# Nine sequences and seven instead of eight and eight: where a Trainium2 kernel splits its expert routing

## The reference, cut to what matters

```python
x = layernorm(x + attention(x))      # 16 heads of 8, alibi bias, causal, output weights
logits = x @ gate_w.T                # 8 experts
probs = softmax(logits); topw, topi = top_k(probs, 2); topw = topw / topw.sum()
routed = sum over the 2 chosen e of topw_e * (silu(x @ gate_e.T) * (x @ up_e.T)) @ down_e.T
shared = (silu(x @ shared_gate.T) * (x @ shared_up.T)) @ shared_down.T
out = layernorm(x + shared + routed)
```

## Time and profile before

| | |
|---|---|
| median of three runs | 1090.53 us (1090.3 to 1091.83) |
| profiled execution, first to last instruction (nothing is shown of what lies around it) | 1172.6 us |
| first unit of sequence 0 | 61.56 us into the span |
| rounds of sequences 1 to 8 | 36.1 to 36.2 us each |
| round of sequence 9, with the routing | 46.91 us |
| first step of the experts | 655.82 us |
| last step of the experts | 1150.71 us |

### The profile page before, as it was taken

The page is one execution under the profiler, slowest core; times in us unless marked ns, Lnnn a source line. Parts: engine busy times, 40 slices in busy tenths (PEclk is TensorE's granted clock), DMA queues, the critical chain, the costliest instruction groups (busy, mean ns, idle before and its releaser), DMA issues. The chain is left out here.

```text
span 1172.6 us, 27905 instructions
## 1 busy us (share of the span) xinstructions
PE 1049.2 (89%) x9236; PEld 724.0 (62%) x9236; DVE 761.8 (65%) x1861; ACT 738.6 (63%) x1630; POOL 634.6 (54%) x1133
## 2 busy tenths in 40 slices
PE   3999999999999989999997898766879999899993
PEld 1445455555455435454543787666769999899882
DVE  3888888888888888888951484221213334566596
ACT  1167887778777667778786344433336777677653
POOL 1045545545455448778877256655654444455542
PEclk9789999999999989999999899878779999999997
DMA  5233233243333314343321511111212223344343
GB/s 139 68 90 100 77 85 90 76 109 86 84 82 78 107 54 112 94 131 89 93 62 49 216 36 47 59 56 57 60 54 61 64 54 87 88 122 120 113 132 94
DMA packets 123243, 101.84 MB, mean 87 GB/s; under 512 B 18736, under 2 KB 113846, under 8 KB 122450
## 3 DMA queue, kind: packets, MB, share of 16 engines
q1 hardware_dynamic: 113362, 78.18, 25.1%
q0 software_dynamic: 8640, 16.87, 4.5%
q10 hardware_dynamic: 1104, 5.01, 1.1%
HBM read 39.31 MB, written 35.66 MB: 64 GB/s over the span
## 5 line engine op out<-in xcount | busy, mean ns | idle before, releaser
L711 ACT ACTIVATE probs<-scores 128x512 f32<-128x512 f32 x640 | 355.4, 603 | 78.3 <-PE scores L620 73.7
L779 POOL TENSOR_SCALAR_AFFINE_SELECT probs<-probs 128x256 f32<-128x256 f32 (+1 forms) x640 | 223.8, 364 | 180.1 <-ACT probs L711 168.2
L1213 DVE TENSOR_TENSOR e_hid<-e_gate,e_up_ps 128x352 f32<-128x352 f32 (+2 forms) x190 | 106.5, 560 | 259.9 <-ACT e_gate L1488 161.1
L916 DVE TENSOR_REDUCE rowmax<-maxed 128x1 f32<-128x512 f32 (+1 forms) x384 | 246.2, 682 | 33.6 <-PE maxed L603 30.2
L597 PE MATMUL maxed<-kstack,qstack 64*128 64x512 bf16 (+3 forms) x1024 | 232.3, 315 | 15.8 <-DMA kstack<-parts 8.5
L620 PE MATMUL scores<-qstack,kstack 64*128 64x512 bf16 (+3 forms) x1024 | 229.2, 303 | 7.2 <-ACT probs L711 6.2
L1571 POOL DMA_INDIRECT y_tokens<-e_raw,e_row_i x142 | 140.2, 987 | 147.7 <-ACT e_raw L1510 116.1
L636 PE MATMUL pv<-probs,vaug 128*32 128x512 f32 (+3 forms) x2048 | 192.7, 449 | 0.4 <-POOL probs L779 0.4
L916 DVE TENSOR_REDUCE maxB<-maxed 128x4 f32<-128x512 f32 x256 | 165.3, 681 | 20.6 <-PE maxed L603 18.6
L620 PEld LDWEIGHTS scores<-qstack,kstack 64*128 64x128 bf16 x1024 | 68.9, 94 | 160.9 <-ACT probs L711 103.9
L603 PE MATMUL maxed<-causal,halves 64*128 64x128 bf16 (+1 forms) x1280 | 162.1, 212 | 0.0
(11 more groups left out here) (185 smaller groups left out, 1568.5 us busy)
## 6 DMA issues: line engine op xcount, KB each, us to landing
qstack<-parts SPq DMA_DIRECT2D x96, 128.0 KB
kstack<-parts SPq DMA_DIRECT2D x96, 128.0 KB
x_sorted<-zeros SPq DMA_DIRECT2D x16, 580.5 KB
e_xs<-x_sorted SPq DMA_DIRECT2D x142, 64.5 KB
e_raw<-y_tokens SPq DMA_DIRECT2D x64, 128.0 KB
xin<-in_x SPq DMA_DIRECT2D x16, 256.0 KB, 3.2
e_group_in<-x1T_all SPq DMA_DIRECT2D x16, 256.0 KB, 3.0
out<-e_raw SPq DMA_DIRECT2D x64, 64.0 KB
```

The lines of the kernel that those rows point to most:

```text
L711: act.activation(probs[g % 2][:, u * T:(u + 1) * T], scores[st.at(0, SEQ_UNITS, UNITS * g + u) % SB][:], ACT.Exp).then_inc(S["exp_done"], 1)
L779: pool.affine_select(out=view, in_=view, compare_op=ALU.is_ge, fill=0.0, base=0, pattern=pattern, channel_multiplier=-1).then_inc(S["maske ...
L916: dve.tensor_reduce(out, keys, AX.X, ALU.max).then_inc(S["max_taken"], 1)
L1213: dve.tensor_tensor(hid[step % len(hid)][rows, 0:cols], gate[step % 2][rows, 0:cols], up_ps[step % 2][rows, 0:cols], ALU.mult).then_inc(S[ ...
```

## The change

The parts become unequal: the first has nine sequences (36 tiles, 79 slots), the second seven (28 tiles, 63 slots). `CTS`, `STARTS`, `CSLOTS` and `ZEROED` hold the numbers of each part, and the sums stay 64 tiles and 142 slots. The rest follows:

- The routing of the first part moves to the round of sequence 10. Its job is split: `rt` (place 25) makes the totals alone and copies them, `rp` (TensorE 29, VectorE 31) makes the other product and `place`. The pieces between go one after each maximum from the 27th on.
- The 72 scatters of the first part: 13 to a round in the rounds 11 to 15 (65), and seven in the experts' steps 8 to 14, one a step, with the semaphore `x_behind`, for which SP waits ahead of the first slot's load.
- 27 steps of the shared expert stand ahead of the slots and 21 behind them. Tokens of the second part are due at 0.74 a step. Mixing starts at step 120 with one tile in 1.25 steps, and for the second part at step 175.
- In both parts the totals' product now comes first, and the experts' routing chain is over 28 tiles.

```diff
-        33: "pv1", 34: "pv2", 35: "x1t", 36: "pv3", 37: "lg"},
+ "PE": ... 25: "pv2 rt", 26: "pv3", 29: "rp", 30: "pv0", ...     "DVE": ... 25: "rt", 31: "rp m", ...
-ROUTE_AT = 9
-SCATTER_AT = (10, 13)
+ROUTE_AT, COUNTED = 10, 12
+SCATTER_FROM, SCATTERS_A_SEQ = 11, 13
-    "rt": ("placed", 0, 1),
+    "rt": ("routed", 0, COUNTED), "rp": ("placed", 0, 1),
-CT = NTILE // CHUNKS
+CTS = (SPLIT_SEQS * QT, NTILE - SPLIT_SEQS * QT)
+STARTS = (0, CTS[0])
+TOKENS_WITHIN = min((B - SCATTER_FROM) * SCATTERS_A_SEQ, 2 * CTS[0])
+TOKENS_BEHIND = 2 * CTS[0] - TOKENS_WITHIN
...
-    dve.wait_ge(S["prefix_ps"], 2)
-    link(dve.tensor_copy(counts[:], prefix[:, CT * NE:2 * CT * NE].rearrange("p (t e) -> p e t", e=NE)))
-    yield
+    dve.wait_ge(S["prefix_ps"], 1)
+    link(dve.tensor_copy(counts, totals.rearrange("p (t e) -> p e t", e=NE)))
+    yield "counted"
...
+    dve.wait_ge(S["prefix_ps"], 2)
+    dve.tensor_tensor(place, prefix.rearrange("p (t e) -> p t e", e=NE),
+                      running.rearrange("p e t -> p t e"), ALU.add).then_inc(S["placed"], 1)
...
-                    if (n + 1) * 11 // SEQ_UNITS > n * 11 // SEQ_UNITS and scattered[choice] < CT:
-                        scatter(pool, keep, dram, 0, scattered[choice], choice, S["x_scattered"])
+                    if n * SCATTERS_A_SEQ // SEQ_UNITS == (n + 1) * SCATTERS_A_SEQ // SEQ_UNITS:
+                        return
+                    scatter(pool, keep, dram, 0, t, choice, S["x_scattered"])
-                pool.wait_ge(S["x_scattered"], 32 * CT)
+                pool.wait_ge(S["x_scattered"], 16 * TOKENS_WITHIN)
...
-                        for _ in range(8):
-                            next(route, None)
+                        next(route)
...
-                        if n < 12 or n >= 30:
+                        if n < 12 or n >= 26:
                             next(route, None)
...
-MIX = ((PARTED + CSLOT + 24, 3, 2), (PARTED + NSLOT + 6, 3, 4))
+MIX = ((PARTED + CSLOTS[0] + 14, 5, 4), (PARTED + NSLOT + 6, 3, 4))
-WRITES_A_STEP, NORM_TAKES, TOKENS_A_STEP = 1.55, 0.7, 0.92
+WRITES_A_STEP, NORM_TAKES, TOKENS_A_STEP = 1.55, 0.7, 0.74
+BEHIND_FROM = 8
...
+                        if n == 0:
+                            sp.wait_ge(S["x_behind"], 16 * TOKENS_BEHIND)
...
+                    if 0 <= step - BEHIND_FROM < TOKENS_BEHIND:
+                        choice, t = divmod(TOKENS_WITHIN + step - BEHIND_FROM, CTS[0])
+                        scatter(pool, keep, dram, 0, t, choice, S["x_behind"])
```

More of the change, by code:

```diff
@@ L224 @@
 NE = 8
+SPLIT_SEQS = 9
 F = 352
@@ L981, in turns_at, with group_bank @@
     return [(chunk, t) for chunk, (first, steps, turns) in enumerate(MIX)
-            for t in range(-2, CT + NORM_LAG) if first + t * steps // turns == step]
+            for t in range(-2, CTS[chunk] + NORM_LAG) if first + t * steps // turns == step]
 def mixed_at(turn, lag):
     chunk, t = turn
-    return chunk * CT + t - lag if 0 <= t - lag < CT else None
+    return STARTS[chunk] + t - lag if 0 <= t - lag < CTS[chunk] else None
+def group_bank(group):
+    return (group + SPLIT_SEQS) % 2
 def quad_at(turn, lag):
@@ L1002, in writes_by_step @@
         room = min(room + WRITES_A_STEP, 2.5) - NORM_TAKES * sum(quad_at(turn, 1) is not None for turn in turns_at(step))
-        due = 2 * CT if step < PARTED else int(tokens_first + TOKENS_A_STEP * (step - PARTED + 1))
+        due = 2 * CTS[1] if step < PARTED else int(tokens_first + TOKENS_A_STEP * (step - PARTED + 1))
         now = [tokens, results]
-        while room >= 1 and tokens < min(due, 2 * CT):
+        while room >= 1 and tokens < min(due, 2 * CTS[1]):
             tokens, room = tokens + 1, room - 1
@@ L1012, in writes_by_step @@
         assert made - results < YTURN
-    assert (tokens, results) == (2 * CT, NSLOT)
+    assert (tokens, results) == (2 * CTS[1], NSLOT)
     return plan
@@ L1095, in experts @@
         picked_in = [sem(f"picked_in{n}") for n in range(TURN)]
-        out_stored = [sem(f"out_stored{n}") for n in range(TURN)]
+        out_stored = keep["out_stored"]
         CONSTS, EXPERTS_IN = 16, 16 * 4
@@ L1155, in _ @@
                             keep_rest(NE, w)
-                route = routing(dve, S, keep, 1, prefix)
+                route = routing(dve, S, keep, 1, prefix[:, 0:CTS[1] * NE], prefix[:, CTS[1] * NE:2 * CTS[1] * NE])
                 by_expert = [P, NTILE, NE]
@@ L1361, in last_chain @@
                         pe.wait_ge(S["chosen"], 1)
-                        tokens = keep["chosen"][:].rearrange("p t e -> p (t e)")
-                        for m, ones in enumerate((keep["before"], keep["onesb"])):
-                            pe.matmul(x_ps[0][:, m * CT * NE:(m + 1) * CT * NE], ones[:], tokens,
+                        tokens, wide = keep["chosen"][:, 0:CTS[1], :].rearrange("p t e -> p (t e)"), CTS[1] * NE
+                        for m, ones in enumerate((keep["onesb"], keep["before"])):
+                            pe.matmul(x_ps[0][:, m * wide:(m + 1) * wide], ones[:], tokens,
                                       start=True, stop=True).then_inc(S["prefix_ps"], 1)
@@ L1659, in build @@
                  "yraw_last": sb("yraw_last", [P, NQUAD, T])}
+        keep |= {"out_stored": [ctx.enter_context(nc.semaphore(f"out_stored{n}")) for n in range(TURN)]}
         attention(nc, io, dram, keep)
```

180 lines of the change are left out of this document (94 added, 86 removed), and 2 rows, old and new, of the table PLACES.

## The result

The changed kernel takes 1094.26 us in the median of 20 runs (1092.44 to 1102.39); the kernel before took 1091.06 us in 20 runs beside it (1088.38 to 1095.71). The ratio is 1.0041, 95% interval 1.0024 to 1.0057; the medians alone are 3.2 us or 0.29% apart, and four runs of over 1100 us pull the ratio up. On another chip it came out at 1.0034 (1.0016 to 1.0051). The forecast was 1094.1 us.

A forecast was written before the change was run, and what follows sets the result against it. The prediction took TensorE to bound plain attention rounds, GpSimd being nearly full in round 15, and the traced slow stretch to be hardly lost untraced. Its terms summed to +3.6 us, 1094.1 us; range 1091 to 1097, over all cases 1085 to 1100.

The forecast's parts named there:

- Rounds 9 and 10: Attention: round 9 loses the routing (-10.7 us), round 10 gets it (+9.7), net -1.0 us (-3.8 to +1.0).
- the rival with round 10 at its floor: Attention: the spread second half costs no clock, so round 10 grows by 6.9 us, not 9.7: 1091.3 us; chance 0.21.
- the rule behind it: The Trainium skill's clock page, read strictly: TensorE that never stands still keeps 2.4 GHz; no size of its own.
- Rounds 11 to 14: Attention: two to three more scatters a round on GpSimd cost +0.6 us in rounds 11 to 13, +0.4 in round 14.
- Round 15: Last attention round: 13 scatters instead of ten on a GpSimd as good as full, +3.1 us (1.5 to 3.7).
- The end of the block: End of the attention: GpSimd waits for a scatter behind the last mask to land, +1.9 us.
- Experts, steps 8 to 14: Seven scatters put GpSimd some 2 us behind, on an input made two steps ahead: +0.4 us (0 to 3).
- First routed step: Experts: its wait for the last weight half goes, with 27 shared steps ahead: -2.3 us (to 0).
- mixing: Experts: 36 tiles bring a ninth group of norms into the routed steps, +0.5 us (0 to 1).
- Dense stretch: Experts' routed steps: the ring and the load hold nobody in untraced runs before either, 0 us.
- The rival on the other side: Experts: the traced loss in the dense stretch is partly real untraced, -4.7 us at the traced price; chance 0.19.
- GpSimd too full: GpSimd's lag in steps 8 to 14 passes its lead and rounds 11 to 14 wait too: 1099 us; chance 0.14.

The follow-up runs named there:

- first trace of before: The kernel before, unedited, in its first traced execution: span 1172.6 us, with a slow stretch in the experts' steps 24 to 70.
- second trace of before: The kernel before, run once more without an edit for another trace: span 1085.3 us, time 1087.03 us.
- first half spread: The changed kernel with the first 12 routing pieces behind every second of the first 24 maxima: 1097.41 us, ratio 1.0048 to the kernel before.
- four together: The changed kernel with experts' scatters in steps 1 to 7, rounds' scatters two units earlier, landing awaited in the experts, first 12 routing pieces spread: 1087.45 us.
- 15 a round: The changed kernel with all 72 scatters in rounds 11 to 15, none in the experts: 1092.89 us, ratio 1.0055 to the kernel before.
- second trace of the changed kernel: The changed kernel run again without an edit, on another chip: span 1092.6 us, time 1093.98 us, ratio 1.0034 to the kernel before.
- three edits: The changed kernel with experts' scatters in steps 1 to 7, rounds' scatters two units earlier, landing awaited in the experts: 1086.81 us, ratio 0.9969 to the kernel before.

## Why the prediction was right

The sum was +3.6 us, and +3.2 and +3.6 were measured. The direction and the main costs (scatters in the last round, the late end of the block) came as said. That the size came out so closely is luck: one step failed by 3.8 us, and others that were put too high gave it back.

- *Rounds 9 and 10*, -1.0 forecast: -1.5 against the first trace of before, +0.9 against the second. Round 10 was put at 45.9 us: 45.39 and 46.31. The size was right, two parts of it weren't. VectorE's extra work is 41.41 - 31.61 = 9.8 us and not 11.5; the second trace of before has 41.47 - 31.67 = 9.8 too, so the wider instructions cost hardly more in all (a typical one went from 0.42 to 0.45 us). And I had TensorE wait a little at each of six maxima; in fact it waits 0.3 us at two of them (449.0 and 451.3) and once long, for a job:

```profile
451.55 0.22 PE L622 MATMUL maxed<-causal,halves 64*128 64x64 bf16 x2
454.62 0.27 PE L542 MATMUL misc<-ident,rowmax 128*64 128x128 f32 x1 [2.85 <-DVE place L342]
```

The transposition of the row maxima (`m`) uses the bank `misc` behind `rp`, and `place` must have read it; `place` stands at the end of the chain in VectorE's queue. So the rival with round 10 at its floor falls, and the rule behind it isn't tested: TensorE did stand still here. I had also misread the first half. The 0.85 us without work between 393 and 396 are not many small waits but the end of one standstill of 1.48 us, of a transposition in the same bank `misc` that waits for VectorE's `k_rest` (392.37 to 393.85 in the first trace of before). In the second trace of before the same standstill, again 1.48 us, brought no drop of the clock. With the pieces spread (first half spread, four together) TensorE waits 0.6 us at this job, and there is no drop. In the second half the clock falls right behind the standstill of 2.85 us, as windows of the changed kernel show:

```profile
451.00:454.00 3.00, 0.47 (x4) 0.20 (x3) 2.90 (x9) 0.38 (x1) 0.36 (x2) 1.00 0.01 3
454.00:457.00 3.00, 2.38 (x19) 0.86 (x19) 2.24 (x5) 1.82 (x5) 1.04 (x2) 0.76 0.05 11
457.00:460.00 3.00, 3.00 (x34) 1.64 (x32) 2.75 (x8) 1.82 (x4) 0.82 (x2) 0.68 0.05 11
```

- *Rounds 11 to 14*, +1.0: 0. GpSimd's idle time covers the scatters; at 15 a round but for 0.3 us in round 13.
- *Round 15*, +3.1, full GpSimd: the sign (no idle before masks) came as said, the length didn't. GpSimd's groups in it:

```profile
L798 POOL TENSOR_SCALAR_AFFINE_SELECT probs<-probs 128x256 f32<-128x256 f32 (+1 forms) x39 | 13.0, 365 | 0.3
L363 POOL DMA_INDIRECT x_sorted<-x_all,place_second x13 | 12.8, 982 | 2.3 <-issue 1.5 <-ACT probs L730 0.7
```

The round is 31.75 us, not 33.5. Its +1.4 is one stretch at low clock, the first window after against the same work before (second trace):

```profile
605.09:609.36 4.27, 4.27 (x29) 0.86 (x32) 0.00 (x0) 2.67 (x6) 3.88 (x10) 0.60 0.74 185
```

```profile
604.67:607.54 2.87, 2.87 (x25) 0.80 (x24) 0.00 (x0) 2.54 (x7) 2.59 (x7) 1.00 1.12 268
```

TensorE is busy throughout in both. In the second trace of the changed kernel this window is at full clock, one at low clock comes 22 us later, and the round is 0.9 us longer than before. GpSimd's own part is what it is late with at the end: the last mask ends 2.81 us behind the last exponential's start (638.64 - 635.83) instead of 1.50 (635.53 - 634.03).
- *The end of the block*, +1.9: the first instruction of the experts' GpSimd comes 8.27 us behind the last mask (646.91 - 638.64) instead of 6.69 (642.22 - 635.53), +1.6; with the late masks (+1.3) and 0.5 from elsewhere, the way to step 7 is 3.4 us longer, 3.2 of them ahead of step 0. Round 15 and this together were put at 5.0 and are 4.8 (4.2 in the second trace of the changed kernel).
- *Experts, steps 8 to 14*, +0.4 (0 to 3): this step failed. It is +4.2, outside its own bounds, and +3.5 to +4.2 in the five traces with the scatters there (22.4 to 23.1 us), against none in the nine without (18.9). I had looked for the wait at GpSimd's input for the shared expert, and asked only who waits for GpSimd's results. VectorE waits for no result of it, and was held all the same.
- *First routed step* -2.3 and *mixing* +0.5: the wait at the first routed step made a step of 4.38 us before, and the step there takes 2.19 now. From step 15 to the end it is -2.9 (-2.2 in the second trace of the changed kernel), forecast -1.8.
- *Dense stretch*, 0: right, as the second trace of before shows. The rival on the other side falls with it. "GpSimd too full" falls at the rounds but names the place, steps 8 to 14, where most was lost. Its mechanism, a late input to TensorE, isn't the one found. Its 1.5 + 1.5 + 2 us were also less than the bounds that it names: 1.9 over the forecast for rounds 11 to 13, 2.0 for round 14 and 2.6 for the steps make 1101 and not 1099.

Against the second trace of before the terms are off by +1.9 (round 10), -2.7 (rounds 11 to 15), +1.5 (end of the block), +3.8 (steps 8 to 14) and -1.1 (the rest of the experts), together +3.4. Some 2.4 of that is the short round 9 of that trace. The failed term was offset by the scatters, which cost less in the rounds than I had them cost, and by the rest of the experts; nothing in the forecast foresaw that.

The range's upper end, 1100, was passed by four of the 20 runs (1100.3 to 1102.4). A lower mean clock goes with these: 0.961 to 0.965 in the four, 0.967 to 0.971 in the other 16. As an estimate, 1091.7 x (1 - 0.971) = 31.7 us went to the clock in the profiled run and 1100.6 x (1 - 0.963) = 40.7 in one of the four, +9.0 where the spans differ by 8.9; for another of them (1100.2, 0.961) it is +11.2 for 8.5. Where they are lost isn't known, since none was traced. Fifteen a round has such runs too (1097.7 to 1100.3, clock 0.961), but its traced one, with 17 us at half clock in round 15, is one of its faster ones (1090.47) and doesn't show what the long ones add.

## What to carry to other kernels

When work is moved onto an engine, look not only for who waits for its results but also for who runs beside it: VectorE's smallest instructions stood still until GpSimd's had ended. A last long-latency DMA at the end of a block should be awaited where its data are read, not where the block ends; that, two masks behind the last scatter and the place of seven scatters were worth 7 us together here, twice what the change cost. And take a second trace before a stretch of the first one is explained.

## What the runs showed of the hardware that I had not expected

- **The low clock outlasts its cause by very different times.** Around the same standstill of 2.85 us the granted clock fell to 1.2 GHz and stayed there for 3.4 us in one trace of the changed kernel, 6.8 in the other, 17 with three edits, though TensorE had no long idle time after the standstill. The round with the routing takes 44.5 to 48.6 us over all traces, and the next one 36.2 to 40.2; this is also the likeliest reason why the runs of one kernel spread over 4 to 12 us, which no trace shows. What decides how long it lasts is open.
- **A low clock without a long standstill.** The first 3 us of round 15 were at a clock of 0.50 to 0.61 in eight traces and at 1.00 in six, though TensorE was busy throughout in the window of the changed kernel above (ahead stands one wait of 0.47 us, and the same in the second trace of before, where the clock didn't fall); in the two traces of the changed kernel it was there once, and once 22 us later. One of the four traces with 11 scatters a round had it and seven of the ten with 13 or 15, which is too few to call the scatters its cause.
- **VectorE and GpSimd.** An instruction of eight columns took 0.17 us alone, and 2.78 when it started beside a scatter of GpSimd that two of its products followed at once.
- **A meeting of the engines costs 5.6 us** behind GpSimd's last instruction (5.56, 5.63, 5.64 in three kernels; 6.21 in one where TensorE came late), 1.5 more if GpSimd waits for a scatter's landing there.
